# Moving the key products of a 16-head attention stage ahead of the first scores, two units early

## What is computed

```python
q = (layernorm(x) @ Wq).reshape(B, 512, 16, 128)      # per batch of 4
k = (ctx @ Wk).reshape(B, 512, 16, 128)
v = (ctx @ Wv).reshape(B, 512, 16, 128)
q, k = rmsnorm(q, gq), rmsnorm(k, gk)
attn = softmax(q @ k.T / sqrt(128))                    # per head
x = x + tanh(g) * ((attn @ v).reshape(B, 512, 2048) @ Wo)
```

## Time and profile before

| | |
|---|---|
| median of three runs | 3538.88 us |
| the profiled execution: its time | 3549.66 us |
| its span, first to last instruction | 3547.6 us |
| mean granted TensorE clock | 0.957 |
| busy: PE / DVE / ACT / POOL | 88% / 74% / 51% / 40% |
| the attention stage (units 0 to 15) | 1510.7 to 2824.9 us of the span |

### The profile page before, as it was taken

How to read it: one execution, slowest core, us unless ns; L and a number is a source line. 1 busy time by engine, 2 the same in 40 slices (tenths; PEclk the granted TensorE clock), 3 DMA queues, 4 the chain that set the end, 5 groups by cost and what they waited for, 6 DMA issues and landing times. The chain is left out here.

```text
span 3547.6 us, 42725 instructions
## 1 busy us (share of the span) xinstructions
PE 3130.4 (88%) x14213; PEld 1831.5 (52%) x14244; DVE 2623.1 (74%) x3494; ACT 1801.9 (51%) x3414; POOL 1416.0 (40%) x956
## 2 busy tenths in 40 slices
PE   7869788999996888699999999999999777998985
PEld 3337544333333555455555555555555356786663
DVE  7855698877765888478777877787777764766886
ACT  5644343666653445465666566655555332664220
POOL 1122288000000000076777777767767544223440
PEclk9879999999998999999999999999999888999997
DMA  4137745222218300255555454445444346665321
GB/s 131 47 117 271 266 121 129 66 57 57 57 30 169 41 1 1 83 175 158 173 172 173 157 172 161 160 157 179 165 158 138 119 166 202 241 249 205 142 72 59
DMA packets 229748, 478.65 MB, mean 135 GB/s; under 512 B 36239, under 2 KB 69647, under 8 KB 213664
## 3 DMA queue, kind: packets, MB, share of 16 engines
q1 hardware_dynamic: 223296, 459.19, 40.9%
q0 software_dynamic: 6240, 16.81, 1.4%
HBM read 387.51 MB, written 92.06 MB: 135 GB/s over the span
## 5 line engine op out<-in xcount | busy, mean ns | idle before, releaser
L2378 POOL TENSOR_TENSOR l2x_inflow<-l2x_dtu,l2x_rows_b 128x512 f32<-128x512 f32 x256 | 419.4, 1638 | 271.2 <-DVE l2x_state L2267 263.0
L178 POOL TENSOR_TENSOR ln_work<-ln_work,minus_half 128x4 f32<-128x4 f32 (+1 forms) x34 | 33.2, 976 | 1037.4 <-DVE ln_work L166 1037.3
L2267 DVE TENSOR_TENSOR_SCAN l2x_state<-l2x_decay,l2x_inflow 128x512 f32<-128x512 f32 x256 | 383.1, 1497 | 16.8 <-ACT l2x_decay L2141 16.8
L1324 DVE TENSOR_REDUCE l1x_mx<-psum 128x2 f32<-128x1024 f32 x256 | 308.3, 1219 | 100.0 <-PE psum L1166 98.5
L2394 POOL TENSOR_TENSOR l2x_y_sum<-l2x_y_sum,l2x_state 128x512 f32<-128x512 f32 x224 | 354.4, 1582 | 33.0 <-DVE l2x_state L2276 33.0
L2076 ACT ACTIVATE l2x_probs<-psum,l2x_soft,l2x_norms 128x512 f32<-128x512 f32 x256 | 195.5, 775 | 320.2 <-DVE l2x_soft L2206 320.2
L1281 ACT ACTIVATE l1x_split<-psum 128x1024 f32<-128x1024 f32 x256 | 262.0, 1025 | 158.7 <-PE psum L1166 158.6
L2276 DVE TENSOR_TENSOR l2x_state<-l2x_state,l2x_rows_c 128x512 f32<-128x512 f32 x256 | 266.8, 1042 | 7.6 <-DMA l2x_rows_c<-l3x_xd_dram 1.1
L126 PE MATMUL psum<-l2x_probs_t,l2x_v_tok 128*128 128x512 f32 x512 | 236.3, 605 | 28.9 <-ACT l2x_probs_t L212 25.9
L126 PE MATMUL psum<-l2x_xt,l2x_wq 128*128 128x512 f32 x512 | 230.9, 594 | 7.7 <-issue 6.2
L126 PE MATMUL psum<-l2x_kt,l2x_qt 128*128 128x512 f32 x512 | 230.5, 593 | 4.0 <-ACT l2x_probs L2076 4.0
(11 more groups left out here) (458 smaller groups left out, 7199.6 us busy)
## 6 DMA issues: line engine op xcount, KB each, us to landing
l2x_rows_b<-l3x_xd_dram SPq DMA_DIRECT2D x256, 256.0 KB, 3.7
l2x_rows_c<-l3x_xd_dram SPq DMA_DIRECT2D x256, 256.0 KB, 3.7
l2w_raw<-l_w SPq DMA_DIRECT2D x38, 1024.0 KB, 7.0
l2x_wkv<-l2x_kv_dram SPq DMA_DIRECT2D x32, 1024.0 KB, 6.9
l2w_raw<-l_w SPq DMA_DIRECT2D x38, 512.0 KB, 4.5
l1x_heads_dram<-l1x_stage SPq DMA_DIRECT2D x32, 512.0 KB, 3.3
l2x_wq<-l_wq SPq DMA_DIRECT2D x16, 1024.0 KB, 7.2
l2x_wo<-l_wo SPq DMA_DIRECT2D x16, 1024.0 KB, 5.3
```

The source lines that it names most:

```text
L1324: main.drain(dve.tensor_reduce(mx[:, gg % 2, :, j, t], g["psum"][:, b:b + 2, :], AX.X, ALU.max), f"m{n}_0", banks=2)
L2267: dve.tensor_tensor_scan(state[:, s % KEPT, :], decay[:, s % 3, :], inflow[:, s % 3, :], 0.0, ALU.mult, ALU.add).then_inc(scan_done, 1)
L2378: pool.tensor_tensor(inflow[:, s % 3, :], dtu[:], rows_b[:, s % 3, :], ALU.mult).then_inc(inflow_ready, 1)
```

## The change

The key products of unit u+2 are made in iteration u behind the output products of unit u, so that those of unit u+1 are there before `score(u, 0)`; the turned x of a new batch is made ahead of that output. The two first sets of keys and the first turned x are made ahead of the loop or in its first iteration. On ACT the key drains go to the end of an iteration behind the last decay, the decays 0 and 1 ahead of the first exponentials, `turn(u, 0)` ahead of `query(u + 1, 0)`. On DVE maxima and biases of head 1 go ahead of scan 2, the copies of the turned x behind the turned keys. On SP the load of the next query weight goes from step 15 to step 13. POOL's order is unchanged.

```diff
--- before.py
+++ after.py
@@ -1792,7 +1792,11 @@
 
 def l2_jobs():
 
-    jobs = []
+    def front(u):
+        turned = [(f"xt{u // G2}_{c}", "act" if c % 2 else "dve") for c in range(DC)] if u % G2 == 0 and u < NU else []
+        return turned, [(f"k{u}_{t}", "act") for t in range(ST)] if u < NU else []
+
+    jobs = front(0)[0] + front(0)[1]
     for u in range(-1, NU):
         pre, on = u + 1 < NU, u >= 0
 
@@ -1808,11 +1812,7 @@
         def query(h):
             return [(f"q{u + 1}_{h}", "act")] if pre else []
 
-        jobs += score(0)
-        if (u + 1) % G2 == 0 and pre:
-            jobs += [(f"xt{(u + 1) // G2}_{c}", "act" if c % 2 else "dve") for c in range(DC)]
-        jobs += [(f"k{u + 1}_{t}", "act") for t in range(ST)] if pre else []
-        jobs += score(1) + query(0) + turn(0) + query(1) + value(0) + turn(1) + score(2) + value(1) + query(2)
+        jobs += score(0) + score(1) + query(0) + turn(0) + query(1) + value(0) + turn(1) + score(2) + value(1) + query(2)
         jobs += turn(2) + score(3) + query(3) + value(2)
         jobs += [(f"ssq{u + 1}", "act")] if pre else []
         jobs += turn(3)
@@ -1820,7 +1820,8 @@
         jobs += value(3)
         jobs += [(f"v{u + 1}_{t}", "act") for t in range(ST)] if pre else []
         jobs += [(f"kt{u + 1}_{h}", "dve") for h in range(4)] if pre else []
-        jobs += [(f"out{u}_{t}", "dve") for t in range(ST)] if on else []
+        turned, keys = front(u + 2)
+        jobs += turned + ([(f"out{u}_{t}", "dve") for t in range(ST)] if on else []) + keys
     return jobs
 
 
@@ -1943,7 +1944,7 @@
                     if n == 6 and u + 1 < NU:
                         ring.wait_filled(sp, 0, f"k{u + 1}_{ST - 1}")
                         value_weight(u + 1)
-                    if n == 15 and u + 2 < NU:
+                    if n == 13 and u + 2 < NU:
                         ring.wait_filled(sp, 0, f"q{u + 1}_3")
                         weight(wq, "l2_wq", u + 2, wq_in)
                     row_b(u * NS + n + 2)
@@ -2038,11 +2039,10 @@
                         ring.fill(transpose_group(pe, bank(f"kt{u}_{h}"), [k_tok[:, t, h * P:(h + 1) * P]
                                                                            for t in range(ST)], g["ident"][:]))
 
+            x_turned(0)
+            context(0, "k", range(ST))
             for u in range(-1, NU):
                 score(u, 0)
-                x_turned(u + 1)
-                context(u + 1, "k", (0, 1))
-                context(u + 1, "k", (2, 3))
                 score(u, 1)
                 query(u + 1, 0)
                 turn(u, 0)
@@ -2062,8 +2062,9 @@
                 value(u, 3)
                 context(u + 1, "v", range(ST))
                 keys_turned(u + 1)
-                output(u, (0, 1))
-                output(u, (2, 3))
+                x_turned(u + 2)
+                output(u, range(ST))
+                context(u + 2, "k", range(ST))
 
         @blk.scalar
         def _(act):
@@ -2141,18 +2142,18 @@
                 act.activation(decay[:, s % 3, :], dt[:, u % 2, :], ACT.Exp,
                                scale=g["a_neg"][:, u % G2, n:n + 1]).then_inc(decay_ready, 1)
 
+            x_turned(0)
+            context(0, "k", k_tok)
             for u in range(-1, NU):
+                decays(u, 0)
+                decays(u, 1)
                 exponent(u, 0)
-                decays(u, 0)
-                x_turned(u + 1)
-                decays(u, 1)
-                context(u + 1, "k", k_tok)
                 decays(u, 2)
                 exponent(u, 1)
                 decays(u, 3)
+                turn(u, 0)
                 query(u + 1, 0)
                 decays(u, 4)
-                turn(u, 0)
                 query(u + 1, 1)
                 decays(u, 5)
                 inverse(u, 0)
@@ -2182,6 +2183,8 @@
                 decays(u, 13)
                 decays(u, 14)
                 decays(u, 15)
+                x_turned(u + 2)
+                context(u + 2, "k", k_tok)
 
         @blk.vector
         def _(dve):
@@ -2282,20 +2285,20 @@
                     dve.scalar_tensor_tensor(tile, tile, g["skip"][:, u % G2:u % G2 + 1], y_sum[:, u % 2, :], ALU.mult,
                                              ALU.add).then_inc(y_read, 1)
 
+            x_turned(0)
             for u in range(-1, NU):
                 scan(u, 0)
                 maxima(u, 0)
                 biases(u, 0)
                 gather(u, 0)
                 scan(u, 1)
-                x_turned(u + 1)
                 gather(u, 1)
+                maxima(u, 1)
+                biases(u, 1)
                 scan(u, 2)
                 inverse(u, 0)
                 gather(u, 2)
                 skip_term(u - 1)
-                maxima(u, 1)
-                biases(u, 1)
                 scan(u, 3)
                 gather(u, 3)
                 scan(u, 4)
```

## The result

The changed kernel takes 3566.6 us at the median of five runs (3563.9 to 3573.9), where the kernel before took 3538.9: a ratio of 1.0067, with a 95% interval of 1.0046 to 1.0088. It is slower, by 27.7 us of the medians (16 to 31 by the interval); 27 were forecast. The profiled execution of after took 3568.55 us with a span of 3566.5.

What follows compares the result with a forecast made beforehand. TensorE, busy 1253 of 1314 us, was taken to bound the stage. Units 0 to 14 went from 1238.5 to 15 x 83.8 + 3 x 1.75 + 3.4 = 1265.7, +27, giving 3566 us; range 3524 to 3585.

Steps and rivals of the forecast that it cites:

- Step 1: Keys before score 0 on TensorE: score 0 starts at 19.3 instead of 13.7, DVE waits 4.6 us before maxima 0.
- Step 2: Maxima 1 before scan 2 on DVE: value 0's 1.65 us wait goes, scan 2 ends at 30.0 instead of 24.4.
- Steps 3 and 4: POOL's key power ends at 38.9 instead of 33.2; DVE's bias 2 is late, turn 2 starts 1.6 us later.
- Step 5: Turn 2 to turned norms: exponentials 3 are 2.7 us late, plain units take 83.8 us instead of 81.1.
- Steps 6 and 7: Layer-norm units also take 83.8 us, a gain of 1.9 each; moving the turned x earlier changes nothing.
- Step 8: Moved and delayed loads of weights and C rows: taken as nothing, up to 1.2 us in the range.
- Step 9: Start of the stage: TensorE waits for unit 1's key weight, +3.4 us, once.
- Step 10: Last unit, without keys or power: change taken as 0, within 1 us either way.
- Faster: Rival: port lock costs little, scan 6 to bias 2 takes 8.3 us, not 11.3; units 79.4, 3500 us; chance 0.20.
- No change: Rival: DVE gets the port first at scan 6, winning 1.1 us; units 81.6, total 3533 us; chance 0.20.
- Slower still: Rival: late C row or key weight costs 1.2 us more a unit; units 85.0, 3584 us; chance 0.12.

Runs made afterwards that it cites:

- e1: Changed kernel with POOL's key norms and their power moved from step 3 to step 1; 3583.2 us in one run.
- e2: Changed kernel with gather 0, scan 1, gather 1 ahead of maxima 0 on DVE, scan 2 and gather 2 ahead of maxima 1; 3508.2 us, ratio 0.9926.
- e6: Changed kernel with only gather 0, scan 1, gather 1 ahead of maxima 0 on DVE, scan 2 staying behind maxima 1; 3548.9 us in one run.
- e4: Changed kernel with the value weight loaded at step 9 instead of step 6; 3557.1 us in one run.
- e3: Changed kernel with maxima and biases of head 1 back behind scan 2 on DVE; 3587.8 us in one run.
- e7: e2 with the value weight loaded at step 9, as in e4; 3501.4 us, ratio 0.9907 to the kernel before.
- e5: Changed kernel with POOL's adds to the sum of states cut from 128x512 to 128x4, leaving out most of the sum; 3509.3 us in one run.
- e8: e7 with maxima 0 first again in the four units behind a layer norm and the last unit; 3509.0 us, ratio 0.9917.

## Why the prediction was right

The forecast (3566) and the result (3566.6) are closer than the steps behind them, which err in both directions: the mechanism for the plain units was right, the agreement within 1 us is luck. By its steps, with t of unit 1:

| step | predicted | measured |
|---|---|---|
| 1: score 0 starts; DVE idle before maxima 0; maxima 0 end | 19.3; 4.6; 23.6 | 19.3; 4.57; 23.7 |
| 2: exponentials 1 end; copies of turn 0 end; value 0 | 32.0; 34.6; 35.5 | 32.1; 34.7; 35.8 |
| 3: power ends; inflow 6 ends | 38.9; 40.2 | 39.3; 40.5 |
| 4: bias 2 ends; turn 2 starts | 51.6 to 51.8; 55.0 | 51.9; 55.1 |
| 5: exponentials 3 late by; unit | 2.7; 83.8 | 2.6; 83.7 |
| 6: layer-norm unit without turned x | 83.8 | 83.7 to 84.2 |
| 9: start | +3.4, and 2.0 for unit 0 | +6.9 in all |
| 10: last unit | 0, within 1 | -2.9 |

**Step 1** held in every number. **Step 2** held but for its last sentence: the 1.65 us before value 0 do not go wholly. ACT does the query's square and copy right behind the copies of turn 0, and value 0 waits 0.41 for that copy, which the step had not looked at. **Steps 3 and 4** had their numbers right, except that scan 3 does not run unhindered (2.28 us). They stated the price as the power and inflow 6 being late; e1 shows that nothing is won by moving the power alone, and e2 and e6 that the unit gets shorter as the scans start earlier. The sum was made by shifting a measured stretch of 11.3 us, so it did not depend on which of the two it was. Not forecast was the wait of 1.26 us within score 2, for value 0's product on DVE: its fourth tile wants a bank which DVE has not read yet. It ends at t = 45, and turn 2 waits for exponentials 2 in any case, so it adds nothing; it is why turn 2 itself waits only 1.56: the two together are 2.8, within the 2 to 3.5 us that were named as a sign.

**Step 5** was the one with the widest bounds (79.4 to 85.7), and the rule by which I chose within them held: exponentials 3 late by one turn of the port more than exponentials 2. Their distance was 9.6 us in the earlier trace rows and is 10.4 here, 0.8 more where 1.1 was taken. Units 1 to 14 were to be 21.7 us longer in sum and are 22.9. **Steps 6 and 7** held; the layer norm's wait is covered, and the turned x costs its 1.75.

**Step 8**, the loads: taken as nothing, up to 1.2. Gather 6 waits 0.46 for its C row, and e4, where it doesn't, has the same unit 1 and 3.2 / 14 = 0.23 us less on average over the units. So 0 to 0.5.

**Step 9** was too small: the sum holds 3.4 and 2.0 for unit 0's own lateness (83.8 less 81.8), 5.4 together, and 6.9 were measured. The wait itself was nearly right (3.15), but the product behind it took 7.41 us instead of 5.86, at a granted clock of 0.77. The term of the clock behind a long wait was left out of the sum, and it is the 1.5 us that are missing.

**Step 10** was wrong by its sign, outside of its own bounds. The last unit has no keys of its own. TensorE's waits in its middle, before and under it after:

```profile
2766.09 1.09 PE L119 MATMUL psum<-ident,l2x_soft 128*128 128x128 f32 x4 [6.74 <-ACT l2x_probs L2076]
2771.45 5.16 PE L126 MATMUL psum<-l2x_probs_t,l2x_v_tok 128*128 128x512 f32 x8 [4.26 <-ACT l2x_probs_t L212]
...
2788.85 0.65 PE L119 MATMUL psum<-ident,l2x_soft 128*128 128x128 f32 x4 [1.15 <-DVE l2x_soft L2215]
2793.35 5.40 PE L126 MATMUL psum<-l2x_probs_t,l2x_v_tok 128*128 128x512 f32 x8 [3.85 <-ACT l2x_probs_t L212]
...
2806.18 1.14 PE L126 MATMUL psum<-l2x_kt,l2x_qt 128*128 128x512 f32 x2 [3.10 <-DVE l2x_ot L2221]
```

Before, it waited 6.74 us for exponentials 1; after the change 1.15 us, for the inverse sums, are left there, and value 0 starts at t = 29.3 instead of 35.8. The later waits (a new one of 3.10 within score 2) take back more than half of that. TensorE is busy for the same time in both (56.7 and 56.8), so the 2.9 are waits. They are not all due to the new place of maxima 1: e3, where maxima 1 are back, has the long wait too (6.39 us) and still takes 73.25 us for this unit. So 0.9 of the 2.9 goes with that place and 2.0 with the rest of the change, which no run takes apart.

Added up: 22.9 + 6.9 - 2.9 = 26.9, against 21.7 + 5.4 + 0 = 27.1 of the steps. Units 1 to 14 were 1.2 too low, the start 1.5 too low and the last unit 2.9 too high; these errors cancel by chance.

**The rivals.** *Faster* wanted units of 79.4 because the lock would cost little. It didn't come in after. Its time can be had (e7: 78.9), but by another way than it named: the contended stretch is as long as ever, it only begins earlier. *No change* wanted DVE to win the port at scan 6; DVE waited 1.46 there. *Slower still* wanted late loads; e4 excludes the value weight, and the timeline of after has no wait for a key weight in any unit behind the start.

**The port.** A bias of 128x4 took 1.16 us in turns with POOL and 0.17 alone, and POOL's two small operations on 128x16 took 1.14 and 0.71 in after and 0.22 each in e1 and e3. The Trainium skill ("SBUF — State Buffer", on the shared port pair) has a DVE operation with two SBUF inputs and one of POOL that reads SBUF exclude one another as a whole. The rows of these operations agree, small as they are, and so does e5's DVE, 5.7 us less busy with the same instructions. The power does not agree. These are scan 5 of after, beside the power of 1619.78 to 1623.49, and under it the power and scan 3 of e3:

```profile
1621.42 1.22 DVE L2270 TENSOR_TENSOR_SCAN l2x_state<-l2x_decay,l2x_inflow 128x512 f32<-128x512 f32 x1
...
1616.03 2.91 POOL L2360 TENSOR_TENSOR l2x_norms<-l2x_norms,minus_half 128x16 f32<-128x16 f32 x1
...
1616.88 1.23 DVE L2270 TENSOR_TENSOR_SCAN l2x_state<-l2x_decay,l2x_inflow 128x512 f32<-128x512 f32 x1
```

Both scans lie wholly within a power and take no longer than alone (1.22 at the median). So for this operation the measurement differs from the rule and decides: the power did not keep the scans out for its whole length.

## What to carry to other kernels

When work is moved ahead of something on one engine, look at what the next engine has in its queue at that point: an in-order engine that waits at a head makes everything behind it late, also what is ready. Move ready work into that wait in the same change; here this made the difference between 0.7% slower and 0.7% faster (e2), or 0.9% with the value weight's load moved as well (e7). Judge TensorE's waits by the longest as well as by their sum. And where two engines share a port in turns, look whether a late start can be caught up. Here it was not: in seven kernels of nine the contended stretch took 11.0 to 11.3 us wherever it began. What gained was to enter it earlier; moving one operation out of it (e1) did not.

## What the hardware showed that I had not expected

- One long wait cost more than several short ones of the same sum (4.49 us in e3 and 4.35 in e1 against 4.28 in after). Behind waits of 3.15 us (start of the stage), 3.72 (e1) and 4.28 (e3) the granted clock was 0.77, 0.77 and 0.76 over the 7 us that followed, between TensorE's two levels, 1.2 and 2.4 GHz, and TensorE was busy for 1.2 to 1.6 us more. Behind waits of 1.56 and less in unit 1 of after it stayed at 1.00, and so it did behind the one of 2.59 in unit 2 of e8.
- A POOL operation that is moved out of the contended stretch can make the other engine busier. DVE ran scans beside the power of 128x16 undisturbed (1.22 to 1.24 us); with the power moved away DVE was busy for 2.2 us more (e1). The power takes 3.71 us in after, where a scan is already running at its start, and 2.91 in e1 and e3, where none is.
- Two conditions came together in the loss: with DVE's idle time but fewer and shorter turns of POOL unit 1 takes 80.4 (e5), with the turns but DVE's queue refilled 79.0 (e2), with both 83.7.
